# Loads of group bounds moved, and ScalarE's first expert tile taken out of the loop, in a state-space and mixture-of-experts layer

## The reference

```
u = xn @ W_x.T + b_x ;  g = sigmoid(xn @ W_g.T + b_g)
h = depthwise conv of u over 3 tokens, + conv_b
u = u * g + h * (1 - g)
dt = clip(mean over all tokens of softplus(xn @ W_dt.T + b_dt))
A = -softplus(A_raw) ;  A_d = exp(A * dt) ;  B_d = (A_d - 1) / (A + 1e-6) * B_ssm
state = A_d * state + B_d * u_t ;  y_t = sum over states(state * C_ssm)
attention = layernorm(xn + y @ W_out.T + b_out) * ln_g + ln_b
```

## Time and profile before

| | |
|---|---|
| median of 3 runs | 476.51 us (476.04 to 476.83) |
| the profiled execution | 476.49 us |
| its span | 474.7 us |
| TensorE, matmuls | 419.2 us busy, 88% |
| VectorE | 393.9 us busy, 83% |
| ScalarE | 315.9 us busy, 67% |
| GpSimd | 241.4 us busy, 51% |

### The profile page before, as it was taken

How to read it: one execution, slowest core, us unless ns; L and a number is a source line. 1 busy time by engine, 2 the same in 40 slices (tenths; PEclk the granted TensorE clock), 3 DMA queues, 4 the chain that set the end, 5 groups by cost and what they waited for, 6 DMA issues and landing times. The chain is left out here.

```text
span 474.7 us, 11677 instructions
## 1 busy us (share of the span) xinstructions
PE 419.2 (88%) x3387; PEld 369.6 (78%) x3387; DVE 393.9 (83%) x666; ACT 315.9 (67%) x898; POOL 241.4 (51%) x272
## 2 busy tenths in 40 slices
PE   1047999998998899999999999899998999799991
PEld 1035788886998899999999999799997555478881
DVE  6989676775649999999999999899981459994997
ACT  2686799998776667777665567465666666426873
POOL 4595777777423223333263244643321777776730
PEclk9999999999899989999999999999999999989997
DMA  9997334523121121212231234422112818188544
GB/s 235 260 412 265 103 116 131 164 81 107 52 55 33 33 44 33 44 39 46 65 67 35 42 92 122 101 67 50 39 40 44 223 49 225 52 230 225 161 128 133
DMA packets 111417, 52.78 MB, mean 111 GB/s; under 512 B 48880, under 2 KB 106392, under 8 KB 111384
## 3 DMA queue, kind: packets, MB, share of 16 engines
q1 hardware_dynamic: 106328, 43.48, 35.2%
q0 software_dynamic: 4096, 8.40, 5.8%
q10 hardware_dynamic: 960, 0.52, 0.4%
HBM read 28.12 MB, written 24.25 MB: 110 GB/s over the span
## 5 line engine op out<-in xcount | busy, mean ns | idle before, releaser
L1444 PE MATMUL PS<-AR 128*128 128x128 f32 x1184 | 140.4, 277 | 4.2 <-ACT AR L766 4.2
L1444 PEld LDWEIGHTS PS<-AR 128*128 128x128 f32 x1184 | 137.1, 194 | 5.0 <-ACT AR L766 5.0
L766 ACT ACTIVATE AR<-PS,VC 128x256 f32<-128x256 f32 x296 | 112.2, 489 | 4.7 <-PE PS L1432 4.0
L1430 PE MATMUL PS<-XT,RR 128*128 128x256 f32 x296 | 86.5, 292 | 3.6 <-POOL XT L579 3.4
L1431 PE MATMUL PS<-XT,RR 128*128 128x256 f32 x296 | 83.3, 281 | 0.0
L1432 PE MATMUL PS<-XT,RR 128*128 128x256 f32 x296 | 83.3, 281 | 0.0
L579 POOL TENSOR_TENSOR XT<-XTF,XT 128x256 fp32r<-128x256 f32 x35 | 33.9, 969 | 91.4 <-ACT XT L743 91.4
L573 POOL DMA_INDIRECT sorted_tokens<-RA,posi x64 | 62.2, 971 | 23.7 <-DMA sorted_tokens<-RA,posi 11.3
L603 POOL TENSOR_TENSOR AR<-AR,b2p 128x256 f32 x37 | 36.1, 975 | 56.2 <-ACT AR L779 53.2
L779 ACT ACTIVATE AR<-PS 128x128 f32 x74 | 16.4, 274 | 68.6 <-PE PS L1444 66.2
L1430 PEld LDWEIGHTS PS<-XT,RR 128*128 128x128 f32 x296 | 56.3, 190 | 5.1 <-POOL XT L579 4.7
(11 more groups left out here) (230 smaller groups left out, 859.5 us busy)
## 6 DMA issues: line engine op xcount, KB each, us to landing
sorted_tokens<-AR SPq DMA_DIRECT2D x10, 512.0 KB, 5.7
XSIN<-sorted_tokens SPq DMA_DIRECT2D x160, 32.0 KB
sorted_outputs<-AR SPq DMA_DIRECT2D x37, 128.0 KB, 1.9
RA<-in_L_attn_x_dram SPq DMA_DIRECT2D x8, 512.0 KB, 8.1
normalised_tokens<-RA SPq DMA_DIRECT2D x16, 256.0 KB
RB<-normalised_tokens SPq DMA_DIRECT2D x8, 512.0 KB, 6.9
AR<-in_L_ffn_W_dram SPq DMA_DIRECT2D x15, 256.0 KB, 3.2
out_dram<-RB SPq DMA_DIRECT2D x7, 512.0 KB, 3.3
```

The costliest lines, as they stand in the source:

```text
L766: nc.scalar.activation(HID[n][:, k, :], ps[2 * n + k // 2][:, (k % 2) * FT:(k % 2 + 1) * FT], ACT.Relu, bias=B1C[:, e, k:k + 1]).then_inc( ...
L1430: T.matmul(bank, W1h[slot][:, w], XT[:, 0:FT], start=True, stop=False)
L1444: ins = T.matmul(ps[5 + h][:, 0:D], HID[n][:, k, h * P:(h + 1) * P], W2S[slot][:, k, :], start=(n == 0 and k == 0), stop=(n == 1 and k == ...
```

## The change

The load of the group bounds is put at another place in four streams: GpSimd's from behind the scatters to ahead of its wait for the positions; ScalarE's to ahead of its wait for the positions; TensorE's to behind the first twelve matmuls of the projections; VectorE's from ahead of the gate work to ahead of the last transposes of tiles. SyncE's is left. On ScalarE the last chunk's softplus runs for both halves before the wait for the last projection and the copy of the second expert's weights. ScalarE's first tile is taken out of the loop and written out: relus, placing of tile 1, then the table load for tanh, the first tanh piece, the output copy; the wait for the gate inputs (`s_ge`) stands behind the table load. The loop of group 0 then runs from tile 1.

```diff
--- before.py
+++ after.py
@@ -560,6 +560,7 @@
 
             pool.wait_ge(s_nrm, QT)
             pool.wait_ge(s_nra, QT)
+            bounds = expert_bounds(pool)
             pool.wait_ge(s_pos, 1)
             pool.wait_ge(s_fill, 16 * NZ)
             for t in range(NT + NSLOT):
@@ -579,7 +580,6 @@
                 nc.gpsimd.tensor_tensor(XT[:, FT:2 * FT], XTF[:, slot(i)], XT[:, 0:FT].bitcast(F32), ALU.subtract
                                         ).then_inc(s_xlo, 1)
 
-            bounds = expert_bounds(pool)
             for g in range(E):
 
                 if 1 <= g < E - 1:
@@ -694,6 +694,7 @@
                                          ).then_inc(s_ln[hb], 1)
 
             act.wait_ge(s_vc, 1)
+            bounds = expert_bounds(act)
             act.wait_ge(s_pos, 1)
             softplus(0)
             high(0, 1)
@@ -703,7 +704,6 @@
             nc.scalar.activation(sv[:, :, :], sv[:, :, :], ACT.Exp).then_inc(s_asq, 1)
             act.wait_ge(s_asq, 1)
             nc.scalar.activation(sv[:, :, :], sv[:, :, :], ACT.Ln, bias=1.0).then_inc(s_asq, 1)
-            bounds = expert_bounds(act)
             for i in range(1, NCH // 2 - 1):
                 for s in range(2):
                     high(1 - s, i + s)
@@ -722,12 +722,10 @@
             high_weights(0)
             act.wait_ge(s_tt, 1)
             nc.scalar.activation(XT[:, 0:FT], XTF[:, 0:FT], ACT.Copy).then_inc(s_xtr, 1)
-            softplus(NCH - 1, [0])
+            softplus(NCH - 1)
             act.wait_ge(s_pr[2][HB - 1], NCH)
             high_weights(1)
-            softplus(NCH - 1, [1])
             gate_input(NCH - 1)
-            nc.scalar.preload_act_table_set("exp_and_others")
 
 
             NPIECE = HB * NGATE
@@ -742,9 +740,44 @@
                 act.wait_ge(s_xlo, i)
                 nc.scalar.activation(XT[:, 0:FT], XTF[:, slot(i)], ACT.Copy).then_inc(s_xtr, 1)
 
+            def hidden(g, i):
+                for n in range(2):
+                    e = (g + n) % E
+                    for k in range(KB):
+                        if k % 2 == 0:
+                            act.wait_ge(s_m1[n], i * KB + (k + 2))
+                        nc.scalar.activation(HID[n][:, k, :], ps[2 * n + k // 2][:, (k % 2) * FT:(k % 2 + 1) * FT],
+                                             ACT.Relu, bias=B1C[:, e, k:k + 1]).then_inc(s_re[n], 1)
+
+            def output(i):
+                act.wait_ge(s_m2, i + 1)
+                act.wait_ge(s_yst, i * 16 + 16)
+                for h in range(FH):
+                    ins = nc.scalar.activation(YSB[:, bass.ds((i & 1) * FT + h * D, D)], ps[5 + h][:, 0:D], ACT.Copy, scale=0.5)
+                ins.then_inc(s_ysb, 1)
+
+            for hb in range(HB):
+                act.wait_ge(s_ln[hb], NCH)
+            hidden(0, 0)
+            place_tile(1)
+            nc.scalar.preload_act_table_set("exp_and_others")
             for hb in range(HB):
                 act.wait_ge(s_ge[hb], NCH)
-                act.wait_ge(s_ln[hb], NCH)
+            gate_piece(0)
+            output(0)
+
+            def expert_tile(g, i):
+                hidden(g, i)
+                place_tile(i + 1)
+                if g < 2:
+                    with act.If(i < NPIECE):
+                        gate_piece(nc.s_assert_within(i, 0, NPIECE - 1, skip_runtime_bounds_check_because="the If"))
+                with act.If(i == TEXP):
+                    act.wait_ge(s_earg, 1)
+                    nc.scalar.activation(EX, EX, ACT.Exp).then_inc(s_eexp, 1)
+                    nc.scalar.activation(ER, ER, ACT.Exp).then_inc(s_eexp, 1)
+                output(i)
+
             for g in range(E):
                 if g == 2:
 
@@ -757,27 +790,13 @@
                     act.wait_ge(s_m2, bounds[g])
                     act.wait_ge(s_w1[raw_slot(k)], 16 * raw_loads(k))
                     nc.scalar.activation(W1h[k % 3], W1RAW[raw_slot(k)], ACT.Copy).then_inc(s_wph, 1)
-                with act.Fori(bounds[g], bounds[g + 1]) as i:
-                    for n in range(2):
-                        e = (g + n) % E
-                        for k in range(KB):
-                            if k % 2 == 0:
-                                act.wait_ge(s_m1[n], i * KB + (k + 2))
-                            nc.scalar.activation(HID[n][:, k, :], ps[2 * n + k // 2][:, (k % 2) * FT:(k % 2 + 1) * FT],
-                                                 ACT.Relu, bias=B1C[:, e, k:k + 1]).then_inc(s_re[n], 1)
-                    place_tile(i + 1)
-                    if g < 2:
-                        with act.If(i < NPIECE):
-                            gate_piece(nc.s_assert_within(i, 0, NPIECE - 1, skip_runtime_bounds_check_because="the If"))
-                    with act.If(i == TEXP):
-                        act.wait_ge(s_earg, 1)
-                        nc.scalar.activation(EX, EX, ACT.Exp).then_inc(s_eexp, 1)
-                        nc.scalar.activation(ER, ER, ACT.Exp).then_inc(s_eexp, 1)
-                    act.wait_ge(s_m2, i + 1)
-                    act.wait_ge(s_yst, i * 16 + 16)
-                    for h in range(FH):
-                        ins = nc.scalar.activation(YSB[:, bass.ds((i & 1) * FT + h * D, D)], ps[5 + h][:, 0:D], ACT.Copy, scale=0.5)
-                    ins.then_inc(s_ysb, 1)
+                if g == 0:
+                    with act.If(bounds[1] > 1):
+                        with act.Fori(1, bounds[1]) as i:
+                            expert_tile(0, i)
+                else:
+                    with act.Fori(bounds[g], bounds[g + 1]) as i:
+                        expert_tile(g, i)
 
             def decay(q):
                 if q >= 2:
@@ -1033,7 +1052,6 @@
             step(1, NCH // 2 - 1, last=True)
             split_low(1)
             tiles_to(3)
-            bounds = expert_bounds(dve)
             for hb in range(HB):
                 dve.wait_ge(s_ue[hb], NCH)
             dve.wait_ge(s_ws, 2)
@@ -1213,6 +1231,7 @@
                     tiles_to(36)
             link(ins)
             link(V.tensor_tensor(A32[:, :], AP2[:, 0, :], AP2[:, 1, :], ALU.add))
+            bounds = expert_bounds(dve)
             tiles_to(MAXT + 1)
 
             dve.wait_ge(s_re[0], bounds[E] * KB)
@@ -1387,11 +1406,11 @@
             pe.wait_ge(s_wo, 1)
             pe.wait_ge(s_vc, 1)
             project(0, 0, [0, 1])
+            bounds = expert_bounds(pe)
             pe.wait_ge(s_rkd, 1)
             project(0, 0, [2])
             transpose_chunk(0, 1)
             project(1, 0)
-            bounds = expert_bounds(pe)
             for i in range(1, NCH // 2 - 1):
                 transpose_chunk(1, i)
                 project(0, i)
```

## The result

The changed kernel takes 478.63 us in the median of 22 runs (476.32 to 480.73), the kernel before 475.92 in 22 runs beside them (473.61 to 479.59). The ratio is 1.0052, 95% interval 1.0033 to 1.0071: slower by about 2.5 us, where 2.9 us faster was forecast. The profiled execution of the changed kernel took 479.79, 478.0 of it span, 3.30 more than the profiled one of before. The totals of the page say little: TensorE, VectorE and ScalarE have the same work within 2 us; the granted clock is 0.978 (0.982 before).

What follows compares the result with a forecast made beforehand. The prediction took the tile loop to be set by VectorE's chain from tile 4, with a tie at the end. Its sum was 476.49 - 3.67 - 0.92 + 1.67 = 473.57, forecast 473.6 us, range 471.5 to 476.2.

Steps and rivals of the forecast that it cites:

- What bounds it, and tile 4's path: Tile loop: VectorE's chain sets it, starting at tile 4, which waits for GpSimd's scatters, bounds load and first bias add.
- the 43 that the prediction had named as a sign of being wrong: Scatter stage: the prediction is wrong if GpSimd's scatters start after 43; the first was expected at 41.3 or earlier.
- an open 2.85: Before the positions wait: 2.85 us free for GpSimd's load of 3.3; 0.45 delays the scatters, net gain 2.85.
- Rival (c): At 36.99: three engines' loads go one after the other, GpSimd's ends at 45.2, time 479.3; chance 0.07.
- the term of 3.67: Tile 4 and VectorE's chain come 3.67 us earlier: 2.85 from GpSimd's load and 0.82 from the bias add; bounds 2.2 and 3.67.
- up to 1.2: Bias preparations beside VectorE's two-input add: shared port could hold back up to 1.2 us of gain; not in the sum.
- 0.82: First bias add, before tile 4: takes 0.73 instead of 1.55 as VectorE's two-input add is over; gain 0.82 us.
- the lower bound: TensorE's load in the projection stage: gain 2.17 us from the removed gap at 48.33, with 0 as the other bound.
- ScalarE's edits: Early expert work: TensorE's 1.81 us before its first second-layer matmul goes away; worth nothing in the sum.
- Tile 5, tile 7, the slow clock: Early tile loop: TensorE waits 3 us or more at tile 5, under 0.5 at tile 7, no slow clock behind.
- 0.92: Tile loop: TensorE's lead from no slow clock, 1.72 us, keeps 0.92 past tile 17, shrinking VectorE's idle at tile 30.
- The end: VectorE's load ahead of tiles 36 and 37, priced 2.65, makes the last tile late: cost 1.67 us, bounds 1.1 and 2.72.

Runs made afterwards that it cites:

- the shifted kernels: 32 or 64 unused semaphore increments early in GpSimd's stream: kernel before with GpSimd's load alone at the front, 474.48 and 474.26; changed kernel with 32, 476.18.
- the fourth experiment: Changed kernel with GpSimd's load back behind the scatters and VectorE's back ahead of the gate work: 476.76 us, ratio 0.9998.
- the first experiment: Changed kernel with only GpSimd's load put back behind the scatters: 476.90 us, ratio 0.9986.
- third experiment: Changed kernel with only VectorE's load put back ahead of the gate work: 479.55 us, ratio 1.0051.
- changed kernel with both: Changed kernel with GpSimd's load after the last scatter issued and VectorE's gate work held behind the scatters: 474.61 us, ratio 0.9966.
- fast version: Only TensorE's and ScalarE's edits of the change, gate work held until 62 scatters landed, GpSimd's load behind the last scatter issued: 474.16 us, ratio 0.9942.

## Why the prediction was wrong

**What bounds it, and tile 4's path: right.** In every trace near 476 us, tile 4 follows the last scatter and the bias operations behind it, and the scan stage starts 227.6 to 231.6 behind tile 4. In the changed kernel the store goes out at 133.03, 1.82 later than the earlier trace rows.

**GpSimd's load: the step that failed.** The first scatter started at 45.12, behind the 43 that the prediction had named as a sign of being wrong. The prediction set a load of 3.3 into an open 2.85 and booked +2.85. The bounds were written at 37.53 (36.99 before, the whole run stands 0.5 later there), and the load was over near 44.1 (in the kernel before the first scatter starts 1.04 after what it waits for, and 45.12 - 1.04 = 44.08): 6.5 us. Against the forecast the last scatter came 5.68 - 0.45 = 5.23 later, and 0.26 went with the load removed being 3.0 and not 3.3: 5.49, and tile 4's miss is 1.83 + 3.67 = 5.50. Of the 5.23, 4.24 - 0.45 = 3.79 belong to the first scatter (the fetch, by the shifted kernels: the shift takes away 3.58 with GpSimd's load alone and 3.90 in the changed kernel) and 1.44 to longer scatters. The mistake was to take the price of the load from the three rows where it stood, all in other surroundings, and to bound it only by these: the text called 3.3 GpSimd's own gap. A stream at another place is another stream. Rival (c) gave 479.3 with a chance of 0.07 and named the turning point (a load that ends after 43.3) and the sign rightly; its mechanism, loads in a queue, is refuted.

**The bias operations: the second, smaller miss.** Without the fetch the term of 3.67 would still have been too large. With GpSimd's load alone and 32 increments its first bias operation starts at 124.03, 3.22 earlier than before, but tile 4 at 134.60 is only 2.19 earlier. That operation takes 1.34 instead of 0.46, the first bias add starts 3.14 behind it instead of 1.84 and takes 1.22 instead of the 0.73 assumed: moved forward, they run beside VectorE's two-input passes. The prediction named this, with up to 1.2, and put it at nothing in the sum.

**Not foreseen: the long scatters.** The prediction called the load taken out of VectorE at 118.11 worth nothing. It is worth less than nothing: the gate work starts at 115.33, and its two-input passes at 116.14, 120.70 and 125.06 stand beside scatters of 1.74, 1.67 and 1.51 (the one at 123.05, which began 0.03 ahead of a scatter, did it no harm; in the fourth experiment one at 123.01, as close ahead, went with a scatter of 2.02). The pair of durations in the earlier trace rows that the text used to book 0.82 had the mechanism in it; the scatters are GpSimd's work too, and were not asked about. The load's place is not all that decides: in the fourth experiment it is back and two scatters are long, with the gate work starting at 117.62, against 118.11 in the kernel before. It matters how the passes fall against the scatters. The 0.82 itself came in the changed kernel: 0.71 for the add.

**TensorE's load: the lower bound in this pair.** The gap of 2.17 became 2.99 at 41.37. The granted clock (third number from the end) was 0.50 from 41 to 44, and the transposes of the next chunk pair start at 48.71 instead of 48.33. Gain nothing, where 2.17 was taken; it did not matter to the sum, as the text said. But this pair compares unlike clocks. The changed kernel, then the first experiment, which has the same TensorE stream:

```profile
41.00:44.00 3.00, 2.63 (x6) 2.05 (x7) 2.63 (x11) 2.59 (x6) 0.00 (x0) 0.50 0.96 285
```

```profile
40.96 0.47 PE L1401 MATMUL PS<-RR 128*128 128x512 f32 x1 [3.16 <-issue]
```

```profile
41.00:44.00 3.00, 3.00 (x15) 2.50 (x16) 2.85 (x12) 2.94 (x7) 2.19 (x2) 1.00 0.88 268
```

There the clock stayed up and VectorE's last split of weights starts at 112.64, against 114.34 in the kernel before, whose clock stayed up as well. With a low stretch in both, it is 114.36 (changed kernel) against 115.90 (VectorE's load alone, 0.56 from 49 to 52). At like clock the move gives 1.5 to 1.7 in the projection stage. It does not reach tile 4, which hangs on the scatters.

**ScalarE's edits: as said.** The 1.81 before the first second-layer matmuls is gone, and the fourth experiment shows no gain from it (0.9998).

**Tile 5, tile 7, the slow clock: right, but for its size.** TensorE waits 4.95 at tile 5 (3 or more was said) and 0.22 at tile 7 (under 0.5); the clock in 167 to 171 is 1.00 instead of 0.57, and 0.50 now in 152 to 156. VectorE's idle time at tile 30 fell from 1.56 to 0.39. But 1.10 came up at tile 31, at 318.37, so 0.21 was gained and not 0.92. TensorE's row from 230 to 290 is 58.77 busy, with 514 matmuls, against 60.00 and 528; 1.14 of this is its wait at tile 17 (232.80), where the kernel before has none: the lead does end there, as the prediction said.

**The end: the mechanism right, its size by luck.** Gap 3.27 instead of the priced 2.72, TensorE's wait 1.97, cost 1.66 against 1.67. Other pairs of traces with and without this load, from tile 4 to the scan start, give 0.7 (changed kernel, third experiment), 0.8 (VectorE's load alone, kernel before), 1.0 (first and fourth experiment) and 1.3 (changed kernel with both, fast version), and no pair of ratios tells it from nothing.

So 473.57 became: 476.49 + 1.83 - 0.21 + 1.66 = 479.77, against 479.79 measured. One term carries 5.5 of the 6.2 us. The 479.79 is the profiled execution; the median, 478.63, lies 1.2 lower, and outside the range as well.

## What to carry to other kernels

When a step is moved along an engine's stream, price it at its new place: ask what runs there (transfers, the other engines) and whether the engine has instructions at hand, since a burst of small instructions can outrun their fetch, and a shift of the stream by some unrelated instructions, earlier and in idle time, is a cheap test for that cause: load, place in time and traffic stay as they are. The cover to look for is a wait that is already on the path at the same engine: the wait for the last landing took the load (one line, 1.5 us), the wait for the positions took it only once its instructions were at hand. And an engine that comes early to its next work is not neutral if that work slows a neighbour that is on the path.

## What the runs showed of the hardware

- GpSimd's load of eight numbers with its checks took 3.0 us behind the scatters, with a DMA share of 0.00; 6.5 ahead of them; 1.67 or less of idle time in one trace, and 3.56 in another with the same stream. Once its instructions were there it was hidden between the bounds and the positions (first scatter 41.16).
- The fetch of the next block of instructions is a transfer like others: with a DMA share of 1.0 to 1.1 it came about 1.6 us later than with almost none.
- Scatters of 0.96 us took 1.2 to 2.0 when they began during one of VectorE's passes with two inputs in SBUF, and 0.95 to 1.09 in the changed kernel when the gate work was held.
- TensorE's pause of 2.99 ahead of 41.37 went with a clock of 0.50 (1.2 GHz) from 41 to 44; a pause of 3.16 ahead of 40.96, in the first experiment, went with 1.00. The old pause of 2.17 to 2.19 ahead of 48.3 to 48.6 was followed by 1.00 from 49 to 52 in the kernel before and by 0.56 in another trace. So the pause alone does not decide.
- What follows the scan start took 109.07, 110.66 and 112.23 us in traces with no, one and two stretches of the lower clock in it: about 1.6 us for each. The changed kernel's trace, 110.68 with none in it and one just ahead, is an exception.
